# The bound behind the expert weights' scales: sums of squares accumulated on ScalarE in place of maxima reduced on VectorE

## What is computed

```
mod = silu(c) @ wmod                                # shifts, scales and gates for both halves
h = layernorm(x) * (1 + ca) + sa
q, k, v = relu(h Wq + bq), relu(h Wk + bk), h Wv + bv
s = gamma * s + outer(k_t, v_t); z = gamma * z + k_t      # a scan over the tokens
x = x + ga * (q_t s) / (q_t z + eps)
h = layernorm(x) * (1 + cb) + sb
e = argmax(h Wr + br)
x = x + gb * (relu(h W1[e]^T + b1[e]) W2[e]^T + b2[e])
```

## Time and profile before

| | |
|---|---|
| time, median of 3 runs | 466.65 us (466.51 to 466.78) |
| the profiled execution | 469.77 us, its span 467.5 us |
| attention stage | from about 19 to 217 us of the span |
| routing | to about 247 us |
| expert tiles | to the end |
| busy: PE, PEld, DVE | 439.2, 392.0, 385.9 us |
| busy: ACT, POOL | 305.1, 260.2 us |
| mean granted clock of PE | 0.977 of full speed |

### The profile page before, as it was taken

One profiled execution on the slowest core, in us unless ns is written; L12 is line 12 of the kernel. 1 busy time (PEld: TensorE's weight loads), 2 busy tenths in 40 slices (PEclk: granted clock), 3 DMA queues, 4 the chain that ended last, 5 costly groups with the idle time before them and its releaser, 6 DMA issues.

```text
span 467.5 us, 13656 instructions
## 1 busy us (share of the span) xinstructions
PE 439.2 (94%) x4296; PEld 392.0 (84%) x4296; DVE 385.9 (83%) x1012; ACT 305.1 (65%) x804; POOL 260.2 (56%) x429
## 2 busy tenths in 40 slices
PE   7999999999999999995767999999999999999992
PEld 4898889999889988893436999989999999999991
DVE  2548999999999999999985887787887777888862
ACT  1335666666666666664606877878777888778870
POOL 2112577777667766756346465656656556664332
PEclk9999999999999999997779999999999999999997
DMA  8725344444444444411015243443333443442110
GB/s 281 254 81 175 119 159 158 158 158 153 152 147 153 156 157 147 136 47 68 25 32 141 59 104 76 110 100 88 87 85 90 87 116 78 97 58 57 45 29 2
DMA packets 43572, 51.71 MB, mean 111 GB/s; under 512 B 24811, under 2 KB 37356, under 8 KB 41328
## 3 DMA queue, kind: packets, MB, share of 16 engines
q1 hardware_dynamic: 37552, 36.67, 27.1%
q0 software_dynamic: 4992, 12.60, 9.8%
q10 hardware_dynamic: 960, 1.57, 1.0%
HBM read 35.22 MB, written 13.50 MB: 104 GB/s over the span
## 4 chain that ended last, share of the span: by engine, by line
PE 76%; DVE 13%; issue 3%; DMA 3%; DVEq 2%; ACT 1%; POOL 1%; ACTq 0%; POOLq 0%
PE ps_o L1434 17%; PE ps_qk L1351 11%; PE ps_qk L1420 9%; PE ps_va L1420 9%; PE ps_va L1361 6%; PE ps_o L1310 5%; PE ps_kv L1317 5%; PE ps_va L1338 3%; PE ps_o L1306 3%; DVE w L1123 2%; DMA w<-in_wmod 2%; DVE arena L1109 2%; PE ps_k L1189 2%; DVEq L1127 1%; PE ps_x L1231 1%
## 5 line engine op out<-in xcount | busy, mean ns | idle before, releaser
L1434 PE MATMUL ps_o<-w,arena 128*128 x936 | 108.7, 273 | 0.6 <-DVE arena L1109 0.4
L1434 PEld LDWEIGHTS ps_o<-w,arena 128*128 128x128 f16 x936 | 89.8, 98 | 10.9 <-issue 1.2
L1123 DVE COPY w<-w 128x2048 f16 x78 | 59.2, 760 | 34.5 <-PE ps_va L1420 23.9
L660 ACT ACTIVATE arena<-ps_qk,arena 128x128 f32<-128x128 f32 x156 | 44.6, 368 | 41.9 <-PE ps_qk L1420 39.1
L1351 PE MATMUL ps_qk<-arena,wqk_b 128*128 128x128 f32 x512 | 62.4, 275 | 0.0
L1420 PE MATMUL ps_qk<-arena,w 128*128 128x128 f16 x936 | 58.7, 219 | 3.6 <-DVE w L1123 1.9
L544 POOL DMA_INDIRECT out_rows<-arena,slot_token x39 | 42.1, 1081 | 34.5 <-POOL arena L540 30.6
L1351 PEld LDWEIGHTS ps_qk<-arena,wqk_b 128*128 128x128 f32 x512 | 59.7, 192 | 0.0
L1420 PEld LDWEIGHTS ps_qk<-arena,w 128*128 128x128 f16 x936 | 55.2, 98 | 5.3 <-issue 2.4
L1420 PE MATMUL ps_va<-arena,w 128*128 128x128 f16 x936 | 58.6, 219 | 0.2 <-DVE w L1123 0.2
L1109 DVE TENSOR_TENSOR arena<-arena 128x512 f16<-128x512 f32 x78 | 53.3, 683 | 4.7 <-ACT arena L668 3.7
(11 more groups left out here) (192 smaller groups left out, 834.2 us busy)
## 6 DMA issues: line engine op xcount, KB each, us to landing
w<-in_w_raw SPq DMA_DIRECT2D x16, 1024.0 KB, 5.1
token_rows<-arena SPq DMA_DIRECT2D x64, 128.0 KB, 1.9
arena<-in_x SPq DMA_DIRECT2D x32, 128.0 KB, 2.1
b_sb<-in_b2b SPq DMA_DIRECT2D x1, 1024.0 KB, 5.3
w<-in_wmod ACTq DMA_DIRECT2D x1, 768.0 KB, 8.7
w<-in_wqkv SPq DMA_DIRECT2D x1, 768.0 KB, 8.1
arena<-token_rows,slot_token POOLq DMA_INDIRECT x39, 3.6
out_rows<-arena,slot_token POOLq DMA_INDIRECT x39
```

The lines of the kernel that those rows point to most:

```text
L660: last = act.activation(hid[:, f, :], bank[("qk", "va")[h]][:, (f % 4) * P:(f % 4 + 1) * P], ACT.Relu, bias=consts_now[:, r, f:f + 1], sca ...
L1123: dve.tensor_copy(now[:, :, i * F // 2:(i + 1) * F // 2], of[:, :, i * F // 2:(i + 1) * F // 2]).then_inc(s_w1, 1)
L1434: last = pe.matmul(bank[f"o{n % 2}"][:, 0:D], hid_parts[:, r % 2, b, f, :], w[:, bass.ds(m, 1), a, f * D:(f + 1) * D].rearrange("p a d -> ...
```

## The change

`max_piece` and its calls go: DVE reduces no weights. ACT gets `square_half` at the end of each slot (k, u) with k from 0 to 15: it waits in u = 0 for the matrix to have landed, squares half of matrix k (128 x 1024 fp32), adds the squares up along the row into one column of `w_piece` with `accum_out`, and writes the squares themselves as fp16 to a place that nothing reads (`squares`). `w_piece` has three columns per matrix instead of five. PE's L1335 waits for both halves of a matrix. DVE's L967 adds the three sums where it took the largest of five. `scale_matrix` halves the exponent of the sum of squares by a shift of 24 and builds the two scales from it, in three instructions as before. The floor that stands for the bias is squared, one instruction more, once, in `token_scale`. `HID_SCALE` becomes 2^-20.

The diff, cut to its core:

```
-        w_piece = sb("w_piece", [P, NM, 5])
+        w_piece = sb("w_piece", [P, NM, HALVES + 1])
...
+        squares = gate_b.bitcast(F16)
...
+            def square_half(k, u):
+
+                if (m := matrix_at(k, MAX)) is not None:
+                    if u == 0:
+                        act.wait_ge(s_wraw, 16 * (m + 1))
+                    need(act, s_wboth, HALVES * m + u)
+                    half = raw_w[:, landing(m), u * (MW // HALVES):(u + 1) * (MW // HALVES)]
+                    act.activation(squares, half.rearrange("p (b c) -> p b c", b=B), ACT.Square,
+                                   accum_out=w_piece[:, m, u:u + 1]).then_inc(s_wboth, 1)
...
                 hi_piece(k, u, 1)
+                square_half(k, u)
...
-                floors = w_piece[:, 1:NM:2, PIECES]
-                step(dve.tensor_scalar(floors, b1_all, hid_unit, 2.0 / P, ALU.mult, ALU.mult))
-                dve.tensor_scalar(floors, floors, 2.0 ** -60, None, ALU.max).then_inc(s_floor, 1)
+                floors = w_piece[:, 1:NM:2, HALVES]
+                step(dve.tensor_scalar(b1_max, b1_all, hid_unit, 2.0, ALU.mult, ALU.mult))
+                step(dve.scalar_tensor_tensor(floors, b1_max, 1.0 / P, b1_max, ALU.mult, ALU.mult))
+                dve.tensor_scalar(floors, floors, 2.0 ** -100, None, ALU.max).then_inc(s_floor, 1)
...
-            def max_piece(k, u, j):
...
-                scale_of(w_most, w_scale[:, m:m + 1], w_unscale[:, m:m + 1], s_wbits, m, s_wscale)
+                dve.tensor_scalar(bits.bitcast(I32), w_most.bitcast(I32), 24, None,
+                                  ALU.arith_shift_right).then_inc(s_wbits, 1)
...
-                        dve.tensor_reduce(w_most, bank["va"][:, W_AT:W_AT + PIECES + 1], AX_X, ALU.max).then_inc(s_wmax, 1)
+                        dve.tensor_reduce(w_most, bank["va"][:, W_AT:W_AT + HALVES + 1], AX_X, ALU.add).then_inc(s_wmax, 1)
...
-                max_piece(k, u, 0)
...
-                max_piece(k, u, 1)
...
-                        pe.wait_ge(s_wboth, m + 1)
+                        pe.wait_ge(s_wboth, HALVES * (m + 1))
```

More of the change, by code:

```diff
@@ L60 @@
 EXP_ONE = 1 << 23
-HID_SCALE = 2.0 ** -23
+HID_SCALE = 2.0 ** -20
 W_AT = DV + P
@@ L125 @@
 PIECES, STAGES = 4, 4
+HALVES = 2
 def build(nc, x, wqkv, wv_rows, bqkv, gamma, wr, brb, w_raw, b1, b2b, c_t, wmod, consts, out):
@@ L720, in _ @@
             step(dve.tensor_tensor(c_silu, c_sb, c_exp, ALU.mult))
-            dve.memset(w_piece[:, :, PIECES:PIECES + 1], 2.0 ** -60)
+            dve.memset(w_piece[:, :, HALVES:HALVES + 1], 2.0 ** -100)
             dve.memset(small[:, 50:51], 0.0).then_inc(s_csilu, 1)
@@ L887, in scale_matrix @@
                 dve.wait_ge(s_wmax, m + 1)
-                scale_of(w_most, w_scale[:, m:m + 1], w_unscale[:, m:m + 1], s_wbits, m, s_wscale)
+                dve.tensor_scalar(bits.bitcast(I32), w_most.bitcast(I32), 24, None,
+                                  ALU.arith_shift_right).then_inc(s_wbits, 1)
+                dve.wait_ge(s_wbits, m + 1)
+                dve.tensor_scalar(w_scale[:, m:m + 1].bitcast(I32), bits.bitcast(I32), float(-EXP_ONE),
+                                  float((TOP + 190) * EXP_ONE), ALU.mult, ALU.add)
+                dve.tensor_scalar(w_unscale[:, m:m + 1].bitcast(I32), bits.bitcast(I32), float(EXP_ONE),
+                                  float((64 - TOP) * EXP_ONE), ALU.mult, ALU.add).then_inc(s_wscale, 1)
             hops = [0]
@@ L1331, in slot @@
                     if u == 0 and (m := matrix_at(k, MAX + 1)) is not None:
-                        pe.wait_ge(s_wboth, m + 1)
+                        pe.wait_ge(s_wboth, HALVES * (m + 1))
                         if m == 1:
                             pe.wait_ge(s_floor, 1)
-                        pe.matmul(bank["va"][:, W_AT:W_AT + PIECES + 1], con("ones"), w_piece[:, m, :], start=True,
+                        pe.matmul(bank["va"][:, W_AT:W_AT + HALVES + 1], con("ones"), w_piece[:, m, :], start=True,
                                   stop=True)
```

## The result

The changed kernel takes 482.64 us (480.96 to 485.93, 4 runs) against 466.71 us (466.51 to 469.45, 4 runs), a ratio of 1.034 with a 95% interval of 1.027 to 1.041. The forecast was 483.2. Its profiled execution has a span of 483.6 us against 467.5: 16.1 us more. Lines of the changed kernel are numbered some 2 to 13 higher; the weighing matmul is L1341 in it, the projections L1357, q and k out of PSUM L615 and L619, the hi parts L582, the squares L569.

A forecast was written before the change was run, and what follows sets the result against it. PE was taken to bound the attention stage, DVE close behind; waits for ACT's second square summed to 13.5 us plus 15 r = 3.0, so 466.65 + 16.5 = 483.2 us, range 479 to 488.

The forecast's parts named there:

- What bounds the stage: In the attention stage PE sets the period of 11.89 us, DVE follows closely, and time taken from DVE is worth next to nothing.
- The rival by LDWEIGHTS share and occupancy: Attention stage: DVE is the bound, PE's real need is 10.70 of 11.89 us; relieving DVE could give 450 us; chance 2%.
- The 11.89 us period: One attention period of two slots, read from PE's L1351 intervals: 6.06 us with L1335 between, 5.83 without.
- the balance of matrices 2 to 13: Added time in the steady steps: 12 x (0.86 + r) = 10.3 + 12 r.
- The new wait: At L1335 PE waits for ACT's second square: loop of 6.92 + r against 6.06, 0.86 + r per matrix; chance 85%.
- r: Cost on ACT of getting the accumulated sum into `w_piece`, on top of the square: 0.2 us, range 0 to 0.35.
- The first square fits: After slot (k, 0) ACT's queue takes 5.4 us against 5.83 between two starts of L603, 0.4 us to spare.
- DVE's relief at nothing: Removing DVE's 64 reductions, 42.9 us of busy time, gains nothing in steady periods, only old PE waits of 0.35 and 1.30.
- Matrices 14 and 15: Last two L1335 waits for ACT's second square: 2.0 + r and 1.1 + r, after 0.5 and 0.6 off for lighter DVE.
- The busy times: Sign over the whole kernel: DVE's busy time at least 43 us less, ACT's about 40 more.

## Why the prediction was right, and where it was off

*What bounds the stage.* Right. Without DVE's reductions the interval is 6.05 and the time 0.6% lower; it isn't 450 us. The rival by LDWEIGHTS share and occupancy falls with this: DVE's 11.86 us stood above the 10.70 of weight loads, and DVE was not the bound. But one argument for it was unsound. I wrote that a queue that waits for another engine would not repeat to the hundredth. PE's queue does: its interval is 7.03 or 7.04 us in all twelve steps in which it waits for ACT, and 6.60 with half a square. The run without the reductions settles the point, the repetition doesn't. The 11.89 us period that I took as general was a little optimistic: four of the fifteen intervals were 6.26, where DVE's routing work (`choose`) made the maxima late. One of them stands in the earlier trace rows itself, 113.41 to 119.67; I had read it as 0.03 us of waiting and it is 0.20. It made the balance of matrices 2 to 13 0.8 us too high.

*The new wait.* Right in place, cause and nearly in size. Predicted 0.86 + r = 1.06 us a matrix, measured 7.03 - 6.06 = 0.97. All terms but one held: 1.99 from L1357 to L615, 2.39 to the second L582, 0.61 to the square, 0.88 from the end of the read to L1357 (111.19 to 112.07). The term that was off is the square with its sum: 1.25 predicted, 1.17 measured (110.02 to 111.19). The record lengths, 1.07 and 0.22, were within 0.02 of those taken; but the read begins 0.12 us before the square's record ends. The prediction had priced it at its whole length and said that it can't overlap the square. The run without sums gives the same 0.1 from the other side, the run with half a square the slope.

*The first square fits.* Right in the changed kernel: the intervals without a weighing stayed 5.83. The margin was larger than the 0.4 us worked out: ACT is idle for 0.81 us ahead of the next L615 (107.02), since the next operation starts 1.04 us after the square, not 1.25, and L604 0.36 us after L592, not 0.6. Two squares there closed a ring over POOL; I costed that ring too short.

*DVE's relief at nothing.* Right in the steady periods: put back beside the squares the reductions cost 0.3 us in all. At matrices 14 and 15 the prediction took off 0.5 and 0.6 us for it; with the maxima put back the wait for matrix 15 grows by 0.45, that for matrix 14 not at all. There L582 starts 4.26 us after L1357 with the maxima or without, against 4.67 before, so those 0.4 us did not come from a lighter DVE.

*Matrices 14 and 15.* The waits were predicted at 2.2 and 1.3 with r = 0.2 and came to 2.3 and 1.2. What I missed is what follows two waits of 2 us: half clock for a while, 1.5 us after the first and 1.7 us after the second. The kernel before had only the second, of 1.30 us; its clock fell too, but only 2.4 us after the wait, when no more than a part of the last L1310 was left to slow.

So the total is right partly by errors that cancel. Matrices 2 to 13 were put at 12 x 1.06 = 12.7 and gave 10.9: 1.1 too much by the read that overlaps, 0.8 by the late maxima of before. Against that stand 3.2 us of half clock that no step held, and against those again 1.7 us less at the start and from routing on, which I did not pursue: 16.5 - 1.9 + 3.2 - 1.7 = 16.1. The mechanism is what the rows show; the agreement to half a us is luck.

*The busy times.* DVE fell by 36 us, not by 43 or more, and ACT rose by 32, not by 40. Records of neighbours overlap at their ends, which a product of count and mean leaves out: with and without the 64 reductions the changed kernel has DVE busy for 384.2 and 349.3 us, so they cover 35 us and not 42.9.

## What to carry to other kernels

A step moved to an engine with room is paid by where it stands in that engine's queue: find the latest input of the operations ahead of it and the first waiter behind it, and add up that chain. Here the change cost 16 us with the 32 squares at the end of ACT's slot, and with the same squares in gaps of the same slot it gained 2.4, of the 3.3 that leaving the reductions out is worth.

When two engines both look full, neither the busy share nor an even beat tells which of them sets the pace: a queue that waits in every period beats as evenly as one that never waits, and a delay of 0.2 us can stand without an idle time in the row. Take the work of one engine out and read the interval. A variation among equal records (0.41 and 0.21 us for the same 128x8 operation) was the sign in the rows that DVE's busy time held waiting.

## What was not expected of the hardware

- A sum accumulated by ACT is a second record of 0.21 us (32 of them), which starts 0.12 us before the record of the square ends, so it costs about 0.1 us in a chain. The Trainium skill ("ScalarE: Activation LUTs", What ACT_TABLE_LOAD costs) gives 186 ns + 0.833 N for an operation with immediate operands, 1039 ns here; the measured 1066 agree within 3%. No table load was added: one stands in the trace of either kernel.
- PE's granted clock stood at its full level (2.4 GHz) before the wait for matrix 14 and at the half (1.2 GHz) for a time soon after it, in all four profiles in which that wait was 1.87 to 1.99 us; in the profile with a wait of 1.55 us, and in the one with 1.9 us of filler matmuls inside the wait, L1357 took its 1.95 us. The kernel before had it 2.4 us after its wait of 1.30 us at matrix 15. That is one profile for each kernel, two for the changed one, so it shows what happened here and no rule.
- A short DVE operation may carry the length of a POOL operation: L989 of 8 columns had records from 0.19 to 0.70 us. That POOL is the cause is argued from ends that coincide, as said above.
